# An attention and mixture-of-experts kernel: how the probabilities are split and transposed, and how the rotation changes halves

## The chip, the cores and the metric

The kernel runs on 1 core of one Trainium2 chip. The metric is device time in microseconds (us). Before the change three runs took 737.32, 738.01 and 740.93 us; their median is 738.01 us.

## The reference, cut to what matters

`x` is (4, 512, 256). After a layer norm it goes through an attention with 16 query heads and 4 key/value heads of width 128, and through a small mixture of experts; the result is `x + s * silu(ffn)`. The part that the change touches is the attention:

```python
q = q * cos + _rotate_half(q) * sin        # rotate_half: [-x2, x1], halves of 64 change places
k = k * cos + _rotate_half(k) * sin
q = q * xscale;  k = k * (1.0 / xscale)
scores = jnp.einsum('bhqd,bhkd->bhqk', q, k) / scale
scores = jnp.where(causal[None, None], scores, -jnp.inf)
attn = jax.nn.softmax(scores, axis=-1)
out = jnp.einsum('bhqk,bhkd->bhqd', attn, v)
out = out.transpose(0, 2, 1, 3).reshape(B, S, N_HEADS * HEAD_DIM)
return out @ Wo
```

All is float32 in the reference. The kernel keeps precision by splitting each float32 matrix into a float16 part ("hi") and a bfloat16 rest ("lo") and by adding three products: hi·hi, hi·lo, lo·hi.

## The kernel before, in words

The program has two stages. The attention comes first: 16 rounds (4 batches times 4 key/value heads), and in each round 4 heads that share keys and values, so 64 heads. The experts come second, and only their loads overlap the end of the attention.

One head needs scores of 512 queries against 512 keys, causal, so 10 of 16 blocks of 128x128: 1280 columns. They are handled in three units, `SCORE_UNITS`: unit 0 has 512 columns, unit 1 has 384 + 128, unit 2 has 256. For a head the steps are:

- TensorE (`score`, L1390) writes the scores of a unit to one of 3 PSUM banks. It waits until ScalarE has read that bank for the head before (`exped`).
- VectorE (`row_max`, L1096) adds the causal mask and takes the negated row maximum.
- ScalarE (`exponentials`, L777) takes the exponential into SBUF, float32 (`probs`), with the row sums. VectorE inverts the sums (L1102).
- GpSimd (`divide`, L539) multiplies the probabilities by the inverted sums, four instructions a head.
- TensorE (`transpose_probs`, L1403) transposes the ten float32 blocks into two PSUM banks, in three units; ScalarE (`probs_hi`, L785) casts a unit to float16 and VectorE (`probs_lo`, L1108) subtracts to get the low part.
- TensorE (`weigh_values`, L1419) multiplies values by the transposed probabilities, 12 matmuls; ScalarE and VectorE split the output (L799, L1114).

A round also projects the queries and keys of the next round: five items, q0, q1, k, q2 and q3 (`project`, L1359), one of 512 columns each. An item is rotated as follows. VectorE multiplies by cos (L1078) and by sin twice, on 64 partitions each, where the result is written to the other half (L1082, L1083). GpSimd adds (`rotate_sum`, L526), ScalarE casts to float16 (`rotate_hi`, L765), GpSimd subtracts (`rotate_lo`, L533). The first scores of the next round wait for the low part of q0 and of k (`rot_lo`). The item v is projected once (L1374), and the output projection of the round before is four items (L1435), which VectorE adds up (L1121).

The order is written out by hand, one instruction list for each engine, each executed in order; a wait on a semaphore stops all that stands behind it on that engine. In the loop of TensorE: scores of head j+1, then (for j = 1 and 2) the transposes of head j, a projection, an output projection, the last transposes of head j, and the values of head j-1. At the round's end come q2, an output projection, the transposes of head 3, the values of head 2, the scores of the next round's head 0, q3, and the rest. SyncE issues only loads in the attention, none of them inside the steady loop of the rounds.

## Time and profile before

| what | value |
|---|---|
| median of 3 runs | 738.01 us |
| span of the profiled execution | 735.7 us |
| TensorE busy (matmul) | 659.1 us, 90% |
| VectorE busy | 581.6 us, 79% |
| GpSimd busy | 537.8 us, 73% |
| ScalarE busy | 442.3 us, 60% |
| scores of 64 heads, TensorE L1390 | 116.4 us |
| transposes of the probabilities, L1403 | 93.5 us in 640 matmuls |
| values, L1419 | 118.0 us |
| division, GpSimd L539 | 176.4 us in 256 instructions |
| product with sin in two halves, L1082 and L1083 | 55.4 and 54.7 us |
| all DMA traffic | 50.44 MB |

The profiled execution's span of 735.7 us is 2.3 us below the median of the timed runs; only the span stands beside it. The page divides the span into 40 slices of 18.4 us. TensorE is busy for nine tenths or more of most slices from the ninth to the thirtieth, which is the attention; the slices behind are the experts. A row of `timeline` begins with its start and its duration in us from the start of the span. Instructions of an engine overlap by their tail, so the time that one takes from its engine is the distance from its start to the next start.

### The profile page before, as it was taken

The page shows a single profiled execution, that of the slowest core. Times are in us where ns is not written, and L with a number is a line of the kernel's source. Part 1 is how long each engine was busy: PE and PEld are TensorE (multiplying, and loading weights), DVE is VectorE, ACT ScalarE, POOL GpSimd, SP SyncE. Part 2 cuts the span into 40 slices and gives each one's busy share as a digit, 9 for nine tenths or more (in the row PEclk, how much of TensorE's full clock was granted, in tenths as well). Part 3 has the DMA queues.
Part 4 walks back from the last instruction along what each step waited for, and adds up shares of the span by engine and source line. Part 5 has one row for each costly group of instructions (what it writes and reads, how often), then busy time and mean ns, then how long its engine had stood idle before and what let it go on. Part 6 is the DMA issues. An engine that isn't in the chain of part 4 may idle for free.

```text
span 735.7 us, 17233 instructions
## 1 busy us (share of the span) xinstructions
PE 659.1 (90%) x4994; PEld 460.8 (63%) x4995; DVE 581.6 (79%) x1683; ACT 442.3 (60%) x1205; POOL 537.8 (73%) x588
## 2 busy tenths in 40 slices
PE   3678869789999999999999999999987899999992
PEld 1255546556766667676666766667665577767761
DVE  6988879789999999998999999999876344333378
ACT  3585636465657666575675657668584664555542
POOL 4677777978888887888877888888988993555510
PEclk9899989999999999999999999999998999999996
DMA  9491000500000000000000000000122564665772
GB/s 306 165 301 48 1 0 2 141 22 16 0 14 14 0 14 0 14 7 7 14 0 14 0 14 14 0 14 2 35 70 88 167 117 105 138 141 138 210 285 101
DMA packets 64952, 50.44 MB, mean 69 GB/s; under 512 B 35252, under 2 KB 58260, under 8 KB 64916
## 3 DMA queue, kind: packets, MB, share of 16 engines
q1 hardware_dynamic: 60804, 39.45, 19.3%
q0 software_dynamic: 3840, 10.52, 4.3%
q8 instruction: 20, 0.33, 0.2%
q14 instruction: 16, 0.13, 0.1%
q10 hardware_dynamic: 272, 0.02, 0.0%
HBM read 24.72 MB, written 18.96 MB: 59 GB/s over the span
## 4 chain that ended last, share of the span: by engine, by line
POOL 41%; issue 19%; PE 17%; DVE 13%; ACT 7%; DMA 2%; POOLq 0%; SPq 0%; DVEq 0%
POOL arena L539 16%; PE bank L1546 8%; POOL arena L533 8%; POOL arena L526 7%; PE bank L1576 6%; POOL xs_dram L586 4%; ACT arena L777 3%; POOL compare L582 2%; PE bank L1555 2%; DVE arena L1108 2%; POOL arena L563 1%; ACT arena L785 1%; DVE arena L1082 1%; DVE arena L1083 1%; DVE arena L1078 1%
## 5 line engine op out<-in xcount | busy, mean ns | idle before, releaser
L539 POOL TENSOR_TENSOR arena<-arena,rinv 128x128 f32<-128x128 f32 (+3 forms) x256 | 176.4, 720 | 83.5 <-DVE rinv L1102 83.4
L777 ACT ACTIVATE arena<-bank,nmax 128x512 f32<-128x512 f32 (+3 forms) x256 | 132.5, 535 | 64.6 <-DVE nmax L1096 64.6
L1096 DVE CUSTOM_DVE_ANT_0 bank<-bank,mask_b 128x512 f32<-128x512 f32 (+3 forms) x256 | 118.1, 516 | 14.2 <-issue 14.2
L1390 PE MATMUL bank<-arena 128*128 128x512 f16 (+7 forms) x768 | 116.4, 302 | 5.9 <-POOL arena L533 5.9
L785 ACT CAST arena<-bank 128x512 f16<-128x512 f32 (+1 forms) x192 | 93.3, 522 | 45.1 <-PE bank L1403 43.5
L1359 PE MATMUL bank<-xnT_hi,arena 128*128 (+1 forms) x320 | 111.0, 389 | 9.2 <-DVE arena L1083 4.7
L1419 PE MATMUL bank<-arena 128*128 128x512 f16 (+7 forms) x768 | 118.0, 305 | 0.0
L1403 PE MATMUL bank<-ident_f,arena 128*128 128x128 f32 x640 | 93.5, 277 | 25.5 <-DVE arena L1108 14.5
L1108 DVE TENSOR_TENSOR arena<-bank,arena 128x512 bf16<-128x512 f32 (+1 forms) x192 | 109.0, 595 | 3.9 <-ACT arena L785 1.8
L526 POOL TENSOR_TENSOR arena<-arena 128x512 f32<-128x512 f32 x77 | 98.6, 1281 | 2.5 <-DVE arena L1083 2.2
L1403 PEld LDWEIGHTS bank<-ident_f,arena 128*128 128x128 f32 x640 | 74.0, 142 | 38.9 <-DVE arena L1108 18.3
L1390 PEld LDWEIGHTS bank<-arena 128*128 128x128 f16 (+1 forms) x768 | 66.2, 98 | 48.1 <-issue 7.9
L533 POOL TENSOR_TENSOR arena<-arena 128x512 bf16<-128x512 f32 x80 | 92.5, 1161 | 4.8 <-ACT arena L765 4.8
L1435 PE MATMUL bank<-arena 128*128 (+2 forms) x768 | 94.6, 274 | 1.6 <-DVE logit L1048 1.2
L1419 PEld LDWEIGHTS bank<-arena 128*128 128x128 f16 (+1 forms) x768 | 68.3, 99 | 38.3 <-issue 2.4
L1435 PEld LDWEIGHTS bank<-arena 128*128 (+2 forms) x768 | 75.3, 98 | 19.9 <-issue 1.7
L1283 DVE TENSOR_TENSOR arena<-bank,arena 128x176 f32<-128x176 f32 x80 | 27.2, 340 | 73.3 <-ACT arena L912 71.8
L718 POOL DMA_INDIRECT ys_dram<-arena,row_u x48 | 46.0, 959 | 51.2 <-ACT arena L923 51.2
L765 ACT CAST arena<-arena 128x512 f16<-128x512 f32 x80 | 50.3, 629 | 53.9 <-POOL arena L526 49.3
L1359 PE MATMUL bank<-xnT_lo,arena 128*128 (+1 forms) x160 | 61.9, 387 | 0.0
L1359 PEld LDWEIGHTS bank<-xnT_hi,arena 128*128 (+1 forms) x320 | 31.9, 100 | 45.5 <-issue 8.3
L1082 DVE TENSOR_TENSOR arena<-bank,tab 64x512 f32<-64x512 f32 x80 | 55.4, 693 | 2.2
(147 smaller groups left out, 1158.9 us busy)
## 6 DMA issues: line engine op xcount, KB each, us to landing
xs_dram<-s_sb SPq DMA_DIRECT2D x4, 1548.0 KB, 14.4
stage<-w_gate_up SPq DMA_DIRECT2D x16, 352.0 KB
arena<-ys_dram SPq DMA_DIRECT2D x8, 512.0 KB, 6.5
stage<-w_down SPq DMA_DIRECT2D x16, 176.0 KB
stage<-wq SPq DMA_DIRECT2D x4, 512.0 KB, 8.0
stage<-wo SPq DMA_DIRECT2D x4, 512.0 KB, 6.5
stage<-x SPq DMA_DIRECT2D x1, 2048.0 KB, 10.6
out<-s_sb SPq DMA_DIRECT2D x8, 256.0 KB, 2.1
```

Of the source, the lines that this page charges most:

```text
L526: pool.tensor_tensor(rot_a[buf], rot_a[buf], rot_b[buf], ALU.add).then_inc(rot_add, 1)
L533: pool.tensor_tensor(dst, rot_a[buf], hi, ALU.subtract).then_inc(rot_lo, 1)
L539: ins = pool.tensor_tensor(pr, pr, rinv[:, par, qt:qt + 1].to_broadcast([P, (qt + 1) * P]), ALU.mult)
L777: ins = act.activation(probs[par][:, P_AT[qt]:P_AT[qt] + n], score_bank[u][:, col:col + n], ACT.Exp, scale=-1.0, bias=nmax[:, par, qt:qt + ...
L785: act.copy(pT[j % 2][0][:, at:at + cols], pt_bank[(3 * j + u) % 2][:, 0:cols]).then_inc(pt_hi, 1)
L1096: ins = dve.tensor_tensor_reduce(score_bank[u][:, col:col + n], score_bank[u][:, col:col + n], mask_b[:, S - n:S], -1.0, 3e38, ALU.add, AL ...
L1108: dve.tensor_tensor(pT[j % 2][1][:, at:at + cols], pt_bank[(3 * j + u) % 2][:, 0:cols], pT[j % 2][0][:, at:at + cols], ALU.subtract).then_ ...
L1359: ins = pe.matmul(ps[:], w[a][:, c * chunk:c * chunk + DH], tokens[m][:, c * TOK:c * TOK + S], start=(c == 0 and n == 0), stop=(c == KC - ...
L1390: ins = pe.matmul(score_bank[u][:, col:col + n_k], qT[a][:, j * S + qt * P:j * S + (qt + 1) * P], kT[m][:, 0:n_k], start=(n == 0), stop=(n ...
L1403: ins = pe.transpose(pt_bank[(3 * j + u) % 2][:, col + (qt - kt) * P:col + (qt - kt + 1) * P], probs[j % 2][:, P_AT[qt] + kt * P:P_AT[qt] ...
L1419: ins = pe.matmul(o_bank[:, kt * P:S], v_s[a][:, kt * DH:(kt + 1) * DH], pT[j % 2][m][:, PT_AT[kt]:PT_AT[kt] + n_q], start=(kt == 0 and n ...
L1435: ins = pe.matmul(ps[:, 0:D], heads[a][:, j * S + q * P:j * S + (q + 1) * P], w[m][:, j * D:(j + 1) * D], start=(j == 0 and n == 0), stop= ...
```

## The change: what it does

The row sums are inverted as before, but the division on GpSimd is gone. ScalarE takes the exponential in place in PSUM. Then it writes the high half of the probabilities to SBUF in float16, scaled by the inverted sum (`probs_hi`, four instructions a head), and VectorE computes the low half from PSUM in one `scalar_tensor_tensor` per block row (`probs_lo`, four a head). Both halves are then transposed: the high half by four transposing DMAs a head (10 blocks in all) from SyncE's queue (`transpose_hi`), the low half in 16 bits by TensorE, into a single PSUM bank in two units; ScalarE copies these to SBUF (`pT_lo_out`). The scores have 4 banks instead of 3, and a bank is free once the low half is computed, not once the exponential is taken. In the rotation VectorE multiplies by sin in one instruction of 128 partitions, into one buffer `rot_c`; two DMAs of 64 partitions (`swap_halves`) put the halves in their new places, and GpSimd's sum waits for them. The prologue's rotations stay as they were. SyncE's queue now runs through the rounds too, and the loads of the experts stand between them.

```diff
-PT_UNITS = [[(0, 0)], [(1, 0), (3, 384)], [(2, 0)]]
+PT_UNITS = [[(0, 0), (1, 512), (3, 896)], [(2, 0)]]
-PT_UNIT_COLS = [(0, 512), (512, 512), (1024, 256)]
+PT_UNIT_COLS = [(0, 1024), (1024, 256)]
+SCORE_BANKS = 4
...
+            def transpose_hi(rd, j):
+                h, par = rd.head(j), j % 2
+                if not (isinstance(h, int) and h < 2):
+                    sp.wait_ge(pv, h - 1)
+                for u, unit in enumerate(SCORE_UNITS):
+                    sp.wait_ge(p_hi_ready, h * 3 + u + 1)
+                    sp.sem_inc(hi_seen)
+                    for qt, _ in unit:
...
+                        sp.dma_start_transpose(dst, p_hi[par][:, P_AT[qt]:P_AT[qt] + n].bitcast(BF16)).then_inc(pT_hi_in[par], 16)
+            def swap_halves(rd, name):
+                sp.wait_ge(misc_free, rd.item(name))
+                sp.sem_inc(hi_seen)
+                sp.wait_ge(rot_add, rd.rot(name) - SWAP_BACK[name])
+                half, buf = DH // 2, SWAP_BUF[name]
+                sp.dma_start(rot_b[buf][0:half, :], rot_c[half:DH, :]).then_inc(swapped, 16)
+                sp.dma_start(rot_b[buf][half:DH, :], rot_c[0:half, :]).then_inc(swapped, 16)
...
+            def round_(rd):
+                for j in range(GH - 1):
+                    transpose_hi(rd, j + 1)
+                    if not rd.last:
+                        swap_halves(rd, ("q0", "q1", "k")[j])
...
+                if not rd.last:
+                    swap_halves(rd, "q2")
+                    transpose_hi(rd, GH)
+                    swap_halves(rd, "q3")
...
-            def divide(h, par):
-                pool.wait_ge(inverted, h + 1)
-                for qt in range(QT):
-                    pr = probs[par][:, P_AT[qt]:P_AT[qt] + (qt + 1) * P]
-                    ins = pool.tensor_tensor(pr, pr, rinv[:, par, qt:qt + 1].to_broadcast([P, (qt + 1) * P]), ALU.mult)
-                ins.then_inc(normed, 1)
...
+            def probs_hi(rd, j):
+                h, par = rd.head(j), j % 2
+                act.wait_ge(inverted, h + 1)
+                if not (isinstance(h, int) and h < 2):
+                    act.wait_ge(pT_hi_in[par], hi_landed(rd, j - 2))
+                for u, unit in enumerate(SCORE_UNITS):
                     for qt, col in unit:
                         n = (qt + 1) * P
+                        ins = act.activation(p_hi[par][:, P_AT[qt]:P_AT[qt] + n], score_at(j, u)[:, col:col + n], ACT.Copy,
+                                             scale=rinv[:, par, qt:qt + 1])
+                    ins.then_inc(p_hi_ready, 1)
+
+            def pT_lo_out(h, j, units):
                 for u in units:
                     at, cols = PT_UNIT_COLS[u]
-                    act.wait_ge(pt_ps, h * 3 + u + 1)
-                    act.copy(pT[j % 2][0][:, at:at + cols], pt_bank[(3 * j + u) % 2][:, 0:cols]).then_inc(pt_hi, 1)
+                    act.wait_ge(pt_ps, h * 2 + u + 1)
+                    act.copy(pT_lo[j % 2][:, at:at + cols], pt_bank[:, 0:cols]).then_inc(pt_lo, 1)
...
+                    exponentials(h, j + 1)
+                    pT_lo_out(rd.head(j), j, (0,))
+                    probs_hi(rd, j + 1)
...
+            def rotate_products(rd, name, freed, lows):
+                ps, buf = misc_bank[rd.bank(name)], ROT_BUF[name]
...
+                dve.tensor_tensor(rot_a[buf], ps[:], tab[:, cos, :], ALU.mult)
+                if lows is not None:
+                    probs_lo(*lows, (0,))
+                if not (rd.first and name == "q0"):
+                    dve.wait_ge(swapped, rd.swap(name) - SWAP_DMAS)
+                dve.tensor_tensor(rot_c, ps[:], tab[:, sin, :], ALU.mult).then_inc(misc_free, 1)
...
+                    for qt, col in SCORE_UNITS[u]:
+                        n, at = (qt + 1) * P, P_AT[qt]
+                        ins = dve.scalar_tensor_tensor(p_lo[par][:, at:at + n], score_at(j, u)[:, col:col + n], rinv[:, par, qt:qt + 1],
+                                                       p_hi[par][:, at:at + n], ALU.mult, ALU.subtract)
+                    ins.then_inc(p_lo_ready, 1)
...
-                    if reuse:
-                        pe.wait_ge(exped, h * 3 + u - 2)
+                    if not (isinstance(h, int) and h * 3 + u < SCORE_BANKS):
+                        pe.wait_ge(p_lo_ready, h * 3 + u - (SCORE_BANKS - 1))
...
-                    if not first or j > 0 or u == 2:
-                        pe.wait_ge(pt_lo, h * 3 + u - 1)
+                    if not first or j > 0 or u > 0:
+                        pe.wait_ge(pt_lo, h * 2 + u)
```

Before, SyncE's queue has no row inside the loop of the rounds. Now it has these; this piece is the loop's third head (the transposes of head 3's high half), the swap of k and the swap of q2:

```order
L477 ISA [waits pv]
L482 DMA_TRANSPOSE arena<-arena 128x4x128 [waits p_hi_ready]
L477 REGISTER_ALU
L482 DMA_TRANSPOSE arena<-arena 128x3x128 [waits p_hi_ready]
L482 DMA_TRANSPOSE arena<-arena 128x1x128
L477 REGISTER_ALU
L482 DMA_TRANSPOSE arena<-arena 128x2x128 [waits p_hi_ready]
L485 REGISTER_ALU
L487 REGISTER_ALU [waits misc_free]
L489 DMA arena<-arena 64x512 [waits rot_add]
L490 DMA arena<-arena 64x512
```

`pv` counts the heads whose values TensorE has weighed. The two DMAs of k's swap stand behind the four transposing ones and so behind their wait.

ScalarE in the loop, for j = 1, before (L785 are the casts of the transposed probabilities, L777 the exponentials of the next head):

```order
L785 CAST arena<-bank4 128x512 [waits pt_ps]
L785 CAST arena<-bank3 128x512 [waits pt_ps]
L774 ISA
L777 ACTIVATE arena,rsum<-bank0,nmax 128x512 [waits maxed]
L774 REGISTER_ALU
L777 ACTIVATE arena,rsum<-bank1,nmax 128x384 [waits maxed]
L777 ACTIVATE arena,rsum<-bank1,nmax 128x128
L774 REGISTER_ALU
L777 ACTIVATE arena,rsum<-bank2,nmax 128x256 [waits maxed]
```

and after (L843 the exponentials, L863 the copy of the low half transposed by TensorE, L855 the high half):

```order
L843 ACTIVATE bank2,rsum<-bank2,nmax 128x512 [waits maxed]
L840 REGISTER_ALU
L843 ACTIVATE bank3,rsum<-bank3,nmax 128x384 [waits maxed]
L843 ACTIVATE bank3,rsum<-bank3,nmax 128x128
L840 REGISTER_ALU
L843 ACTIVATE bank0,rsum<-bank0,nmax 128x256 [waits maxed]
L862 ISA
L863 COPY arena<-bank4 128x1024 [waits pt_ps]
L849 REGISTER_ALU
L851 ISA [waits inverted]
L855 ACTIVATE arena<-bank2,rinv 128x512 [waits pT_hi_in0]
L855 ACTIVATE arena<-bank3,rinv 128x384
```

What ScalarE does after its exponentials now stands in front of what VectorE waits for.

VectorE in the loop, for j = 2, behind the row maxima of head 3, before (L1108 the low parts, L1078 to L1083 the products of k):

```order
L1108 TENSOR_TENSOR arena<-bank3,arena 128x512 [waits pt_hi]
L1108 TENSOR_TENSOR arena<-bank4,arena 128x512 [waits pt_hi]
L1075 REGISTER_ALU
L1077 REGISTER_ALU [waits misc_ps]
L1078 TENSOR_TENSOR arena<-bank7,tab 128x512 [waits rot_lo]
L1102 RECIPROCAL rinv<-rsum 128x4 [waits exped]
L1082 TENSOR_TENSOR arena<-bank7,tab 64x512
L1083 TENSOR_TENSOR arena<-bank7,tab 64x512
```

and after (L1201 the low halves, L1154 and L1159 the products):

```order
L1190 RECIPROCAL rinv<-rsum 128x4 [waits exped]
L1152 REGISTER_ALU
L1153 REGISTER_ALU [waits misc_ps]
L1154 TENSOR_TENSOR arena<-bank7,tab 128x512 [waits rot_lo]
L1197 ISA
L1201 SCALAR_TENSOR_TENSOR arena<-bank1,rinv,arena 128x512 [waits p_hi_ready,pt_ps]
L1158 ISA
L1159 TENSOR_TENSOR arena<-bank7,tab 128x512 [waits swapped]
L1201 SCALAR_TENSOR_TENSOR arena<-bank2,rinv,arena 128x384 [waits p_hi_ready]
L1201 SCALAR_TENSOR_TENSOR arena<-bank2,rinv,arena 128x128
L1201 SCALAR_TENSOR_TENSOR arena<-bank3,rinv,arena 128x256 [waits p_hi_ready]
```

The low halves belong to the head whose maxima have just been taken; before, they belonged to the head ahead of it.

## Rows read from the trace of the kernel before

**Rows 1.** The page: span, and busy us of each engine with its instructions.

```profile
span 735.7 us, 17233 instructions
...
PE 659.1 (90%) x4994; PEld 460.8 (63%) x4995; DVE 581.6 (79%) x1683; ACT 442.3 (60%) x1205; POOL 537.8 (73%) x588
```

**Rows 2.** `windows`, one steady round: length, busy us of PE, PEld, DVE, ACT, POOL.

```profile
412.35:443.88 31.53, 31.03 (x242) 21.67 (x239) 29.03 (x85) 20.14 (x58) 25.82 (x30) 1.00 0.02 8
```

**Rows 3.** Timeline of PE: start us, duration us, engine, line, operation.

```profile
429.85 1.04 PE L1403 MATMUL bank<-ident_f,arena 128*128 128x128 f32 x8
430.72 1.79 PE L1419 MATMUL bank<-arena 128*128 128x512 f16 x12
432.68 1.80 PE L1390 MATMUL bank<-arena 128*128 128x512 f16 x12 [0.17 <-POOL arena L533]
...
437.14 1.79 PE L1390 MATMUL bank<-arena 128*128 128x512 f16 x12
...
442.69 0.22 PE L1374 MATMUL bank<-arena,xnT_lo 128*128 x1
442.74 0.28 PE L1374 MATMUL bank<-arena,xnT_hi 128*128 x2
...
444.64 1.79 PE L1390 MATMUL bank<-arena 128*128 128x512 f16 x12
...
451.60 1.79 PE L1390 MATMUL bank<-arena 128*128 128x512 f16 x12
```

**Rows 4.** Timeline of DVE, one head of the same round.

```profile
438.93 0.69 DVE L1096 CUSTOM_DVE_ANT_0 bank<-bank,mask_b 128x512 f32<-128x512 f32 x1
...
440.77 0.69 DVE L1078 TENSOR_TENSOR arena<-bank,tab 128x512 f32<-128x512 f32 x1
...
444.82 0.68 DVE L1114 TENSOR_TENSOR arena<-bank,arena 128x512 f32 x1
445.42 0.68 DVE L1087 TENSOR_TENSOR arena<-bank,arena 128x512 bf16<-128x512 f32 x1
446.02 0.41 DVE L1108 TENSOR_TENSOR arena<-bank,arena 128x256 bf16<-128x256 f32 x1
446.36 0.70 DVE L1096 CUSTOM_DVE_ANT_0 bank<-bank,mask_b 128x512 f32<-128x512 f32 x1
```

**Rows 5.** Timeline of ACT, the same head.

```profile
439.72 0.69 ACT L777 ACTIVATE arena<-bank,nmax 128x512 f32<-128x512 f32 x1 [2.35 <-DVE nmax L1096]
...
441.84 1.07 ACT L785 CAST arena<-bank 128x512 f16<-128x512 f32 x2
442.79 0.65 ACT L765 CAST arena<-arena 128x512 f16<-128x512 f32 x1
```

**Rows 6.** Timeline of POOL, the end of a round.

```profile
429.05 1.26 POOL L526 TENSOR_TENSOR arena<-arena 128x512 f32<-128x512 f32 x1
430.28 2.26 POOL L533 TENSOR_TENSOR arena<-arena 128x512 bf16<-128x512 f32 x2
```

**Rows 7.** `source` of L480, ns min/median/max on SyncE; timeline of SyncE: one plain DMA.

```profile
L480 SPq DMA_TRANSPOSE arena<-xs_dram x48: 1188/1193/4862, 593.6 to 689.1; - x48
...
561.51 0.42 SPq L470 DMA_DIRECT2D stage<-w_down  x1
```

**Rows 8.** `dma`: size and median us from issue to landing.

```profile
out<-s_sb SPq DMA_DIRECT2D x8, 256.0 KB, 2.1
...
stage<-shared_down SPq DMA_DIRECT2D x1, 96.0 KB, 3.7
```

**Rows 9.** `dma` of 630 to 660 us: queue q1, in which 16 transposing DMAs ran.

```profile
q1 hardware_dynamic: 8704, 2.10, 41.6%
```

**Rows 10.** Timeline of PE around its longest wait.

```profile
98.54 0.69 PE L1403 MATMUL bank<-ident_f,arena 128*128 128x128 f32 x2 [4.39 <-DVE arena L1108]
99.02 3.41 PE L1419 MATMUL bank<-arena 128*128 128x512 f16 x12
```

**Rows 11.** `windows` around it: PE busy, granted clock, DMA share.

```profile
96.00:100.00 4.00, 1.46 (x5) 0.55 0.00 0
```

266 lines of the change are left out of this document (150 added, 116 removed).

## The prediction

> **What bounds the kernel now.** I read the page first. The span is 735.7 us and TensorE is busy for 659.1 of it [rows 1]. Then I read one steady round in the windows: TensorE is busy for 31.03 of 31.53 us, VectorE for 29.03, GpSimd for 25.82, ScalarE for 20.14, and the DMA share is 0.02 [rows 2]. So the attention is bound by TensorE's work, with VectorE close behind. Each engine works through its list in order, and the timelines show how the lists interlock. The scores of heads 0, 1, 2 and 3 start at 432.68, 437.14, 444.64 and 451.60 [rows 3]; the steps are 4.46, 7.50 and 6.96 us, and 12.61 remain of the round to the next head 0. That last step is the path of k: k's rotation has to come back before the next head 0 can be scored. It is nearly late already, since the scores at 432.68 waited 0.17 us for GpSimd's low part (L533) [rows 3]. Two loops must therefore be watched besides busy time: head to head, and k's path once a round.
>
> **What the change takes from the busy engines.** Eight float32 transposes take 0.87 us of TensorE (429.85 to 430.72), 0.109 each [rows 3]; there are 40 in a round, 4.35 us. The trace has no 16-bit transpose. Its bounds are 0.055, the pitch of 16-bit matmuls of 128 columns (442.69, 442.74) [rows 3], and the same 0.109. I take 0.055, since shape and operand width agree: 2.2 us saved a round, TensorE at 28.9. VectorE loses one of the two products of 0.7 us with sin, five times a round, 3.5 us; the other becomes one instruction of 512 columns at 0.60 (444.82 to 445.42) [rows 4]. The low half is four instructions in place of three. From 0.60 for 512 columns and 0.34 for 256 (446.02 to 446.36) [rows 4], a column costs 1.0 ns and an instruction 0.08 us, so 384, 128 and 256 columns take 0.47, 0.21 and 0.34: 1.62 a head against 1.54. If the three-operand form lasts as long as the row maximum of 512 columns, 0.69 us [rows 4], it is 0.1 us more an instruction. VectorE comes to about 26 us. ScalarE gains four scaled copies a head and its transposed copies stay: about 27 us. GpSimd drops to 13. No engine is full after the change, so by busy time alone a round would take 28.9 us. What decides is the order.
>
> **The head-to-head loop.** Before, VectorE's low part belonged to the previous head, and a score bank was free after the exponential. Now VectorE takes the maxima of a head, then waits for ScalarE, which takes the exponentials, copies the previous head's transposed low half (1024 columns) and only then writes the high half; then VectorE computes the low half, and only behind that, in order, the next maxima. The two engines alternate and little of it overlaps. The link, from the start of one head's maxima to the next head's:
>
> - maxima to the end of the exponentials: 438.93 [rows 4] to 441.84 [rows 5], 2.91. ScalarE now writes to PSUM; I take the same.
> - the copy of 1024 columns: two casts of 512 take 441.84 to 442.79 [rows 5], 0.95.
> - first high half, 512 columns: 0.6 (the cast at 442.79 lasts 0.65 [rows 5]).
> - low half of unit 0, 0.60; product with sin, 0.60; low halves of units 1 and 2, 1.02 [rows 4].
> - one addition of a projection of 256 columns, 0.34 [rows 4].
>
> That is 7.02, and with three hand-offs of some 0.04 us 7.1. It holds from head 2 to head 3. From head 1 to head 2 VectorE has the output's and v's low parts, 1.20, in place of the addition: 8.0. From head 0 to head 1 ScalarE has a cast of 512 columns, half of 0.95, and a copy of 256, some 0.3, in place of 0.95: 6.9. Before, these steps took 6.96, 7.50 and 4.46. The division, 2.75 us a head on GpSimd, was beside other work and its going is worth nothing here.
>
> **The path of k, once a round.** TensorE's projection of k no longer decides. The swap's DMAs stand in SyncE's queue behind the transposing DMAs of head 3, and those wait for `pv` of head 1, because they overwrite the buffer that head 1's values are read from. Head 1's values stand behind the last two transposes of head 2, and these need the single PSUM bank, which ScalarE frees with the copy of 1024 columns behind head 3's exponentials. From the start of head 3's maxima:
>
> - to the end of the exponentials 2.91, the copy 0.95;
> - two transposes 0.11, head 1's values with their tail 1.79 [rows 3];
> - four transposing DMAs on SyncE's queue. Before shows one of four blocks: 1.193 us of the queue [rows 7]. A plain DMA takes 0.42 [rows 7], so I split this into 0.45 and 0.185 a block; 10 blocks in four DMAs are 3.65. The ends: 4 x 1.19 = 4.8 if the cost is the same for any size, and 1.9 if only data counts: q1 took 41.6% of 30 us for 16 transposes of 128 KB, 0.78 each [rows 9], for 320 KB 1.9;
> - the second swap DMA starts 0.45 later and lands after 2.1 us, as a store of 256 KB does; a small one took 3.7 [rows 8]. Take 2.1, bounds 2.1 and 3.7;
> - GpSimd: the sum 429.05 to 430.28, 1.23; then the low part of q1, which stands ahead, and that of k, two in 2.26 [rows 6];
> - the first scores until VectorE can start, 0.8, half of their 1.79 [rows 3].
>
> The sum is 2.91 + 0.95 + 1.90 + 3.65 + 0.45 + 2.1 + 1.23 + 2.26 + 0.8 = 16.25, with eight hand-offs 16.6, where before the step was 12.61. TensorE has some 4.7 us to do behind head 1's values (q2, an output projection, transposes, head 2's values) and then waits about 5 us for k. Such a wait has a second price: after its wait of 4.39 us at 98.54 the values took 3.41 instead of 1.79 us [rows 3, 10], and the granted clock from 96 to 100 us was 0.55 [rows 11], near the lower of the clock's two levels, 1.2 GHz. I put 0.7 us a round on it, the first scores at half speed beyond what VectorE's first maxima hide. VectorE is stopped too: its sin product of q2 reuses `rot_c` and waits for k's swap, but it has nothing on this path.
>
> **The sum.** 6.9 + 8.0 + 7.1 + 16.6 + 0.7 = 39.3 us a round against 31.53, 7.8 more. Fifteen rounds have a path of k: +117 us. The experts' stage begins later by as much and is otherwise the same, since its loads have more time than before. The profiled execution would go from 735.7 to about 853; the median of the runs shown is 2.3 higher, 855. I forecast 855 us. With 1.9 for the transposes, exponentials into PSUM 0.25 us a head shorter and no loss of clock, a round is 35.9, +66 us, 804. With 4.8 us, 3.7 to landing and 0.1 us more an instruction on VectorE it is 43.3, +177 us, 915. The likeliest case's own range is 810 to 905.
>
> **A rule of the skill.** The one row on a DMA transpose reads from HBM, 128 x 512 elements, four blocks in 1.193 us of queue and 0.78 us of data [rows 7, 9]. The Trainium skill (VectorE: DVE Perf Modes, "Rules for kernel authors") says to transpose 128x128 on TensorE if a PSUM destination is acceptable and by the crossbar DMA otherwise, and its section "The three transpose paths" gives 390 ns for TensorE and 1309 ns for the DMA. Before transposes at 109 ns a block, so the page's figure for TensorE is not met here; if its DMA figure held for each block in a row of them, a head's ten would take 13.1 us, more than a head takes now, by an estimate from that page about 1140 us for the whole. The Trainium skill also says (Advanced Engine Details and Errata, "X-Bar Transpose (TRN2)") that transposing DMAs are as fast as regular ones; by that the term of 3.65 would shrink toward its lower bound and the time toward 825. No row of before has a source in SBUF, so neither is settled by it.
>
> **Rivals.** First, the queue becomes the bound: each block read from SBUF costs what the whole four-block DMA cost, 1.19 us [rows 7]. A head needs 11.9 us of SyncE's queue and a round 47.6 + 5 x 0.9 = 52.1 us, 20.6 more; over 16 rounds 1065 us. For it: no row shows a source in SBUF. Against it: 1.193 covers four blocks. Chance with anything above 915: 0.09. Second, faster: the two loops are covered, because ScalarE and VectorE really overlap across units and the swap is back in time; TensorE's 28.9 us would bound, 2.6 less a round, 16 x 2.6 = 42, 696 us. It decides from the point at which a round's four links sum to less than 31.5, and they would have to lose 7.1 of 38.6. For it speaks only busy time [rows 2]. Chance 0.04. Third, no change: the losses of k's path (4.0) hold but the other links gain, 31.5 again, 738 us: 0.02. Fourth, a mild loss: k's path is 3 to 4 us shorter than summed (DMAs in parallel, low landing), a round of 33 to 35.5 us, 760 to 800 us: 0.06.
>
> **How the numbers follow.** The forecast of 855 has 0.79 within 804 to 915. The range for 8 in 10 is 808 to 920: below it lie the second to fourth rivals and above it the first. What a measurement can tell from no change is about 0.5%, 3.7 us. Faster 0.04, same 0.02, slower 0.94.
>
> **What would show it.** Right: in a steady round TensorE is busy for some 29 us of 38 to 40, with one wait of about 5 us before L1481 released by GpSimd's L610 (`rot_lo`), a fallen clock behind it; VectorE's L1201 waits for ScalarE's L855, and ScalarE's L843 for VectorE's maxima, each about once a head; SyncE waits for `pv`; GpSimd's L603 waits for a DMA. Wrong: if score starts are under 7 us apart and the wait for `rot_lo` is under 1 us; if SyncE's queue is busy all the time (the first rival); or if L482 issues take under 0.3 us each and the round is still long, in which case the step is elsewhere, in VectorE's and ScalarE's alternation.

## The result, and the profile after

The changed kernel takes 940.45 us (median of 4 runs, 938.77 to 941.97) against 737.86 us (737.32 to 740.93) of the kernel before: a ratio of 1.2735, 95% interval 1.2703 to 1.2766. The forecast was 855 us with a range of 808 to 920. The direction was right and the size was not: the kernel is 203 us slower, not 117.

The page of the kernel after, span and busy times, answers to [rows 1]; under it the windows of one steady round (length, busy us of PE, PEld, DVE, ACT, POOL, then granted clock, DMA share, GB/s), which answers to [rows 2].

```profile
span 938.3 us, 18321 instructions
...
PE 676.6 (72%) x4930; PEld 433.9 (46%) x4995; DVE 547.5 (58%) x1672; ACT 544.3 (58%) x1397; POOL 365.0 (39%) x332
```

```profile
464.08:508.46 44.38, 31.28 (x235) 19.52 (x238) 27.08 (x83) 26.45 (x69) 15.06 (x13) 0.96 0.28 65
```

The busy times came out near the forecast: VectorE 27.1 us a round (about 26 was worked out), ScalarE 26.5 (27), GpSimd 15.1 (13; by the prediction's own 2.75 us a head it would have been 14.8). TensorE shows 31.3 instead of 28.9. About 1.0 of that goes with the lower clock (0.96 on the mean): rope_engines below, with the same list on TensorE, shows 30.3 at a clock of 1.00. The transposes themselves are as quick as was taken: eight start at 488.94 and the next work at 489.39, 0.056 us each. The other 1.4 us is probably the way busy time is counted, which takes in the tail of the last matmul of every stretch; this was not followed up. No engine is busy for more than 31.3 of 44.38 us. The time went into waits, as the page of waits of the kernel after shows (engine, what, line, releaser: us in all, times, longest):

```profile
POOL arena L603 <- DMA arena<-arena: 359.7, 71, 16.8
ACT arena L832 <- POOL arena L603: 159.9, 40, 13.5
ACT bank L843 <- DVE nmax L1184: 125.4, 71, 5.6
...
DVE arena L1159 <- DMA arena<-arena: 85.2, 29, 10.2
...
PE bank L1481 <- POOL arena L610: 77.1, 16, 9.1
```

GpSimd's `rotate_sum` (L603) waits for the swap's DMAs, and it passes the wait on: to ScalarE, whose `rotate_hi` (L832) stands in one list with the exponentials and the output's high half, and to TensorE's scores (L1481). VectorE's sin product (L1159) waits for the swap before, because `rot_c` is one buffer.

Heads are best compared by the starts of their row maxima. Here are those of heads 0 to 3 and the next head 0 in the timeline of VectorE after (start us, duration us), to which 438.93 and 446.36 of [rows 4] answer:

```profile
464.08 0.69 DVE L1184 CUSTOM_DVE_ANT_0 bank<-bank,mask_b 128x512 f32<-128x512 f32 x1 [0.94 <-issue]
...
471.99 0.70 DVE L1184 CUSTOM_DVE_ANT_0 bank<-bank,mask_b 128x512 f32<-128x512 f32 x1
...
481.49 0.69 DVE L1184 CUSTOM_DVE_ANT_0 bank<-bank,mask_b 128x512 f32<-128x512 f32 x1
...
488.89 0.70 DVE L1184 CUSTOM_DVE_ANT_0 bank<-bank,mask_b 128x512 f32<-128x512 f32 x1
...
508.47 0.69 DVE L1184 CUSTOM_DVE_ANT_0 bank<-bank,mask_b 128x512 f32<-128x512 f32 x1 [0.94 <-issue]
```

The links are 7.91, 9.50, 7.40 and 19.58 us; the same starts before (433.55, 438.93, 446.36, 453.47, 465.06) give 5.38, 7.43, 7.11 and 11.59. The last link holds 8.0 of the 12.9 us a round. Its chain in the timeline after, rows of several engines put in order of time:

```profile
491.81 1.02 ACT L863 COPY arena<-bank 128x1024 bf16<-128x1024 bf16 x1
492.88 0.28 PE L1494 MATMUL bank<-ident_b,arena 128*128 128x128 bf16 x2 [0.72 <-ACT arena L863]
494.09 0.71 PE L1512 MATMUL bank<-arena 128*128 128x512 bf16 x4
495.01 5.21 SPq L482 DMA_TRANSPOSE arena<-arena  x4
500.47 0.46 SPq L489 DMA_DIRECT2D arena<-arena  x1
500.98 0.59 SPq L490 DMA_DIRECT2D arena<-arena  x1
503.34 1.26 POOL L603 TENSOR_TENSOR arena<-arena 128x512 f32<-128x512 f32 x1 [5.96 <-DMA arena<-arena]
504.56 2.26 POOL L610 TENSOR_TENSOR arena<-arena 128x512 bf16<-128x512 f32 x2
506.97 2.74 PE L1481 MATMUL bank<-arena 128*128 128x512 f16 x9 [5.00 <-POOL arena L610]
```

It is the chain that the prediction named: the copy of the transposed low half frees TensorE's transposes, head 1's values end, `pv` lets SyncE issue the four transposing DMAs of head 3, k's swap stands behind them, then landing, GpSimd's sum, two low parts, the scores. What it got wrong stands in the lines: the four DMAs hold the queue for 5.2 us, where 3.65 was taken. The slow scores behind the wait (nine matmuls in 2.74 us) had been forecast.

The second loss is in the link from head 1 to head 2 (timeline after, POOL, ACT, DVE):

```profile
477.55 1.26 POOL L603 TENSOR_TENSOR arena<-arena 128x512 f32<-128x512 f32 x1 [8.07 <-DMA arena<-arena]
...
478.85 0.62 ACT L832 CAST arena<-arena 128x512 f16<-128x512 f32 x1 [1.23 <-POOL arena L603]
479.37 0.58 ACT L877 CAST arena<-bank 128x512 f32 x1
...
480.27 0.69 DVE L1208 TENSOR_TENSOR arena<-bank,arena 128x512 f32 x1 [0.90 <-ACT arena L877]
```

The swap of q3 stands in SyncE's queue behind the four transposing DMAs of the new head 0 (5.19 us from 469.21 on) and is issued from 474.66 on. It comes back late, so ScalarE's cast of q3 is late, the cast of the output (L877) stands behind it in ScalarE's list, and VectorE's low half of the output (L1208) stands ahead of head 2's maxima. Such a chain was not in the prediction.

Over the whole run the last head's maxima start 208.4 us later (755.40 instead of 546.97), and what follows is 5.8 us shorter. Of the 208.4, 15 rounds account for 201.2, of which 15 x 12.87 = 193.0 by the steady round, and the last three heads add 6.9. The remaining 8.2 lie in the first four rounds, above all in the first (58.4 us against 38.7, with GpSimd's longest wait, 16.8) and the fourth (53.3 against 34.5); the second loses less than a steady one, 7.9. There other transfers stand ahead of a swap in SyncE's queue, as swap_only below shows.

### The profile page after: what moved, and what is told of

The parts are those of the page before. It is cut to its first block, busy times and chain, and to the rows that moved or that the text cites. A ratio compares the mean times of both kernels' runs of the same rounds, so it can differ in the third digit from the quotient of the medians.

```text
span 938.3 us, 18321 instructions
## 1 busy us (share of the span) xinstructions
PE 676.6 (72%) x4930; PEld 433.9 (46%) x4995; DVE 547.5 (58%) x1672; ACT 544.3 (58%) x1397; POOL 365.0 (39%) x332
## 4 chain that ended last, share of the span: by engine, by line
issue 39%; POOL 15%; ACT 13%; PE 13%; DVE 9%; SPq 6%; DMA 3%; ACTq 0%; POOLq 0%; DVEq 0%
PE bank L1639 6%; POOL arena L603 6%; ACT bank L843 4%; SPq L482 4%; PE bank L1669 4%; POOL arena L610 4%; ACT arena L855 3%; POOL xs_dram L655 3%; ACT arena L863 2%; POOL arena L632 2%; DVE arena L1201 2%; DMA arena<-arena 2%; ACT arena L832 1%; PE bank L1648 1%; SPq L507 1%
## 5 line engine op out<-in xcount | busy, mean ns | idle before, releaser
L603 POOL TENSOR_TENSOR arena<-arena 128x512 f32<-128x512 f32 x77 | 98.4, 1277 | 361.9 <-DMA arena<-arena 359.7
L1481 PE MATMUL bank<-arena 128*128 128x384 f16 (+2 forms) x763 | 147.1, 337 | 117.3 <-POOL arena L610 77.1
L843 ACT ACTIVATE bank<-bank,nmax 128x512 f32<-128x512 f32 (+3 forms) x256 | 127.7, 499 | 125.6 <-DVE nmax L1184 125.4
L1481 PEld LDWEIGHTS bank<-arena 128*128 128x128 f16 (+1 forms) x768 | 69.9, 108 | 183.3 <-issue 80.2
L1201 DVE SCALAR_TENSOR_TENSOR arena<-bank,rinv,arena 128x512 bf16<-128x512 f32 (+3 forms) x256 | 128.3, 545 | 41.8 <-ACT arena L855 41.7
L832 ACT CAST arena<-arena 128x512 f16<-128x512 f32 x80 | 50.3, 628 | 164.7 <-POOL arena L603 159.9
L855 ACT ACTIVATE arena<-bank,rinv 128x512 f16<-128x512 f32 (+3 forms) x256 | 115.8, 557 | 0.7 <-DVE rinv L1190 0.7
L1494 PE MATMUL bank<-ident_b,arena 128*128 128x128 bf16 x640 | 58.6, 224 | 60.7 <-ACT arena L863 60.7
L1159 DVE TENSOR_TENSOR arena<-bank,tab 128x512 f32<-128x512 f32 x75 | 51.5, 687 | 86.5 <-DMA arena<-arena 85.2
L863 ACT COPY arena<-bank 128x1024 bf16<-128x1024 bf16 (+1 forms) x128 | 90.1, 704 | 0.6 <-PE bank L1494 0.5
L1508 PE MATMUL bank<-arena 128*128 128x512 f16 (+3 forms) x512 | 84.1, 310 | 1.5 <-DVE arena L1208 1.5
L1494 PEld LDWEIGHTS bank<-ident_b,arena 128*128 128x128 bf16 x640 | 42.8, 100 | 83.1 <-ACT arena L863 69.5
L1208 DVE TENSOR_TENSOR arena<-bank,arena 128x512 f32 (+1 forms) x64 | 44.1, 690 | 60.7 <-ACT arena L877 60.7
L785 POOL DMA_INDIRECT ys_dram<-arena,row_u x48 | 46.0, 959 | 49.9 <-ACT arena L1000 49.9
## 6 DMA issues: line engine op xcount, KB each, us to landing
xs_dram<-s_sb SPq DMA_DIRECT2D x4, 1548.0 KB, 15.1
```

What stands on the lines that cost most here:

```text
L603: pool.tensor_tensor(rot_a[buf], rot_a[buf], rot_b[b], ALU.add).then_inc(rot_add, 1)
L843: ins = act.activation(p, p, ACT.Exp, scale=-1.0, bias=nmax[:, j % 2, qt:qt + 1], accum_out=rsum[:, j % 2, qt:qt + 1])
L855: ins = act.activation(p_hi[par][:, P_AT[qt]:P_AT[qt] + n], score_at(j, u)[:, col:col + n], ACT.Copy, scale=rinv[:, par, qt:qt + 1])
L863: act.copy(pT_lo[j % 2][:, at:at + cols], pt_bank[:, 0:cols]).then_inc(pt_lo, 1)
L1201: ins = dve.scalar_tensor_tensor(p_lo[par][:, at:at + n], score_at(j, u)[:, col:col + n], rinv[:, par, qt:qt + 1], p_hi[par][:, at:at + n] ...
L1481: ins = pe.matmul(score_at(j, u)[:, col:col + n_k], qT[a][:, j % GH * S + qt * P:j % GH * S + (qt + 1) * P], kT[m][:, 0:n_k], start=(n == ...
```

## Experiments

Two theories and two rivals were on record. Theory Q: what costs is the place of the swap in SyncE's queue, behind transposing DMAs. Theory A: VectorE and ScalarE take turns on one head. Rivals: D, the data that the transposing DMAs move slow things in general; L, the landing of a swap costs wherever it stands. Four more came with single runs: F and B (a transposing DMA's price on the queue is fixed, or goes by blocks), W (the queries' swaps hold the round as much as k's) and K (the clock behind TensorE's wait). All times are medians; before took 738 to 740 us beside them.

**rope_engines.** The rotation as in the kernel before, all else as after.

```diff
-                dve.tensor_tensor(rot_c, ps[:], tab[:, sin, :], ALU.mult).then_inc(misc_free, 1)
+                dve.tensor_tensor(rot_b[buf][0:half, :], ps[half:DH, :], tab[half:DH, sin, :], ALU.mult)
+                dve.tensor_tensor(rot_b[buf][half:DH, :], ps[0:half, :], tab[0:half, sin, :], ALU.mult).then_inc(misc_free, 1)
...
-                        swap_halves(rd, ("q0", "q1", "k")[j])
```

> The changed kernel, but the rotation's halves change places as before: VectorE multiplies by sin crosswise with two instructions into three rot_b buffers, and no swap DMA is left. In a steady round of the changed kernel (44.38 us) the starts of the row maxima are 7.91, 9.50, 7.40 and 19.57 us apart. Theory Q (the swap stands in SyncE's queue behind transposing DMAs): from head 3 to the next head 0 the wait for pv, 5.2 us of transposing DMAs, 0.9 of issue and 2.3 of landing leave the path of k, and ScalarE's and VectorE's waits for the swap (159.9 and 85.2 us in all) go; VectorE's longer sin product costs 0.8 us a head. A round of 36 to 39 us, 815 to 860 us in all, against 940. Theory A (VectorE and ScalarE alternate on a head, because the score bank comes free only after the low half, and that alone sets the round): the added 0.8 us a head on VectorE is on the path, 5 x 0.8 x 16 = 64 us more, 950 to 1005 us. Theory D (what costs is the data that the transposing DMAs move, beside everything else): no change within 2%, 920 to 955 us.

Measured: 858.2 us, ratio 1.160 (1.156 to 1.164). Links 8.23, 9.21, 8.35, 13.64, a round of 39.43, a little over the 36 to 39 expected; some rounds take 40.2. The last link lost 5.9 us although VectorE had more to do. A alone and D are out.

**swap_first.** The same instructions as after, but each swap ahead of the transposing DMAs in SyncE's list.

```diff
-                    transpose_hi(rd, j + 1)
                     if not rd.last:
                         swap_halves(rd, ("q0", "q1", "k")[j])
+                    transpose_hi(rd, j + 1)
...
                     swap_halves(rd, "q2")
+                    swap_halves(rd, "q3")
                     transpose_hi(rd, GH)
-                    swap_halves(rd, "q3")
```

> The changed kernel with the same instructions, but in SyncE's list each swap stands ahead of the head's transposing DMAs instead of behind them (q2's and q3's both ahead of the next head 0's). Theory Q: the swap's issue (0.9) and landing (2.3) stay, but the wait for pv and the 5.2 us of four transposing DMAs leave k's path; the transposes of a head start up to 1 us later. A round of 35 to 39 us, 800 to 860 us, some 10 to 20 us below or about the same as with the rotation on the engines, whose VectorE has 4 us more a round. Theory A: no change, 925 to 955 us. Theory D: no change, 925 to 955 us. A theory L (the swap's landing of 2.3 us and GpSimd's wait for it are the cost, wherever it stands): 0.9 + 2.3 us stay and only the queue's 5.2 us go where it counts, once a round: 15 x 5.2 = 78, about 862 us or more.

Measured: 844.2 us, ratio 1.141 (1.138 to 1.144). Links 7.91, 8.71, 7.40, 13.60; a round of 37.62. Nothing but the order in one queue was changed, and 96 of the 203 us went. It is below the 862 that theory L gave, so a landing is not the cost wherever it stands.

**one_transpose.** One transposing DMA of ten blocks a head. It waits for the high half of all three units, and TensorE weighs the values with it in matmuls of 128 columns.

```diff
-                    for qt, _ in unit:
...
-                        sp.dma_start_transpose(dst, p_hi[par][:, P_AT[qt]:P_AT[qt] + n].bitcast(BF16)).then_inc(pT_hi_in[par], 16)
+                sp.wait_ge(p_hi_ready, h * 3 + 3)
...
+                sp.dma_start_transpose(dst, p_hi[par][:].bitcast(BF16)).then_inc(pT_hi_in[par], 16)
```

> The changed kernel with one transposing DMA of ten blocks a head instead of four of one to four blocks; it waits for the high half of all three units, and the values' matmuls with the high half are ten of 128 columns a pass in place of four of 512 to 128 (the same columns). Theory Q with a fixed cost of 1.19 us of queue for each transposing DMA: four take 5.2 us and one takes 1.2 to 1.6, so k's path is 3.6 us shorter and the waits for q2's, q0's and q1's swaps shrink with it: a round of 36 to 40 us, 825 to 875 us. If the cost goes by blocks (0.45 and 0.185 a block, as the prediction split it), one takes 2.3 us against 3.65: 1.35 us a round, 915 to 925 us. If it goes by blocks alone (1.19 for four), 3.0 us for ten: 880 to 910. Theory A: the start is later by the wait for the last unit, not on VectorE's or ScalarE's path: no change, 925 to 950 us. Theory D: no change, the same bytes, 925 to 955 us.

Measured: 860.0 us, ratio 1.162 (1.158 to 1.166), links 7.91, 8.26, 7.40, 15.09. Of the expectations only that of a fixed price fits. The rows of the transposing DMAs in one_transpose and in the kernel after (ns min/median/max of one) show it:

```profile
L479 SPq DMA_TRANSPOSE arena<-arena x64: 1255/1324/8840, 35.5 to 679.8; - x64
```

```profile
L482 SPq DMA_TRANSPOSE arena<-arena x256: 1177/1190/6742, 33.3 to 765.4; - x128
```

**swap_only.** The kernel before with the swap by DMA and nothing else of the change.

```diff
-                dve.tensor_tensor(rot_b[buf][0:half, :], ps[half:DH, :], tab[half:DH, sin, :], ALU.mult)
-                dve.tensor_tensor(rot_b[buf][half:DH, :], ps[0:half, :], tab[0:half, sin, :], ALU.mult).then_inc(misc_free, 1)
+                    dve.wait_ge(swapped, rd.swap(name) - SWAP_DMAS)
+                    dve.tensor_tensor(rot_c, ps[:], tab[:, sin, :], ALU.mult).then_inc(misc_free, 1)
```

> The kernel before with one part of the change alone: the sin product is one instruction into rot_c and two DMAs on SyncE's queue swap the halves; probabilities are divided, transposed in float32 on TensorE and split as before. Nothing stands ahead of a swap in SyncE's queue. Each round has 3.5 us less on VectorE and k's path has 0.9 of issue and 2.3 of landing more, less 0.8 of the product. Before, k's low part was 0.17 us late in a round of 31.53. Theory Q: a landing alone costs little: k's projection came some 3 us ahead of GpSimd's sum of k, which hides most of it: 738 to 765 us. Theory L (the landing is the cost wherever it stands): 15 x 2.4 = 36 us and a lost clock in each round behind the wait, 775 to 800 us. Theory A: 730 to 740 us, VectorE is relieved and nothing alternates.

Measured: 751.7 us, ratio 1.015 (1.012 to 1.019). The windows of a steady round of swap_only:

```profile
449.20:480.54 31.34, 30.64 (x240) 21.70 (x239) 25.17 (x79) 20.15 (x57) 25.83 (x30) 1.00 0.20 50
```

The round is as long as before (31.5) with VectorE at 25.2 instead of 29.0 us: relieving VectorE was worth nothing, TensorE held the round. The 12 us lie in the first round (49.4 us against 38.7) and the fourth (39.7 against 34.5). That nothing stands ahead of a swap, as the expectation says, is not so there. In the first round it is four stores of 1548 KB each from another part of the program (SyncE and GpSimd in swap_only):

```profile
45.04 11.47 SPq L474 DMA_DIRECT2D xs_dram<-s_sb  x4
56.62 5.00 SPq L457 DMA_DIRECT2D arena<-arena  x1
61.67 1.33 SPq L458 DMA_DIRECT2D arena<-arena  x1
68.06 1.26 POOL L568 TENSOR_TENSOR arena<-arena 128x512 f32<-128x512 f32 x1 [10.04 <-DMA arena<-arena]
```

GpSimd's wait of 10.0 us is about the 10.8 that the round lost. In the fourth round loads of the experts' weights fill the queue from 164.34 to 172.03 us, and GpSimd waits 4.8 us for the swap behind them. No run moved these transfers, so this is read from the trace and not tried; it is the same mechanism, a swap behind other DMAs in one queue, without a transposing one.

**k_engines.** After, with k alone rotated on the engines.

```diff
+                if name == "k":
...
+                    dve.tensor_tensor(rot_b[b][0:half, :], ps[half:DH, :], tab[half:DH, sin, :], ALU.mult)
+                    dve.tensor_tensor(rot_b[b][half:DH, :], ps[0:half, :], tab[0:half, sin, :], ALU.mult).then_inc(misc_free, 1)
+                    return
```

> The changed kernel with k alone rotated as before (two crosswise products on VectorE into rot_b, no swap DMA for k); the four queries keep their swaps, each still behind a head's transposing DMAs in SyncE's queue. Theory Q, k's path alone: the wait for pv, 5.2 us of transposing DMAs, 0.9 of issue and 2.3 of landing leave the path from head 3 to the next head 0, VectorE has 0.8 us more: that link falls from 19.57 to 13.6 us as where all five rotations went back to the engines or the swaps stood first, a round to 37 to 39 us, and with 7 us less in each of 15 rounds the kernel takes 835 to 860 us. Theory W (k's path is only a part, and ScalarE's and VectorE's waits for the queries' swaps, 159.9 and 85.2 us in all, hold the round as much): more than half of the gain stays away, 885 to 925 us. Theory A (alternation of VectorE and ScalarE on a head alone): 940 to 955 us.

Measured: 852.4 us, ratio 1.155 (1.152 to 1.158); links 7.29, 9.50, 7.40, 14.17. k's path carries nearly all of it. The link of 9.50 stays, as it must where it is the queries' swaps that are late; with the swap first or with one transposing DMA it fell to 8.7 and 8.3. (In rope_engines, without swaps, it is 9.2, because the sin products take longer there: its link without any late swap, from head 2 to head 3, is 0.95 longer too.)

**engines_and_one.** rope_engines and one_transpose together.

> The rotation on the engines as in the kernel before, and one transposing DMA of ten blocks a head. Alone the first gave 858.2 us and the second 860.0. Theory Q says that both take the same thing off k's path, the queue ahead of the swap; with no swap left the transposing DMAs only have to be back before the values, two heads later. So the two do not add: 845 to 865 us. If the gains were of different causes they would add, 80 + 82: about 780 us. Theory D (the transposing DMAs' load on anything beside the swap costs): clearly under 845.

Measured: 857.3 us, ratio 1.161 (1.158 to 1.163), a round of 39.72. The gains don't add: both took the same queue off k's path.

**order_as_before.** engines_and_one with the exponentials in SBUF and VectorE's maxima ahead of the low half. What comes with that changes too: three banks for scores and two for the low half's transposes, those transposes one head later, and one buffer instead of two for the high half and for the transposed low half.

```diff
-                        p = score_at(j, u)[:, col:col + (qt + 1) * P]
-                        ins = act.activation(p, p, ACT.Exp, scale=-1.0, bias=nmax[:, j % 2, qt:qt + 1], accum_out=rsum[:, j % 2, qt:qt + 1])
+                        n = (qt + 1) * P
+                        ins = act.activation(probs[j % 2][:, P_AT[qt]:P_AT[qt] + n], score_at(j, u)[:, col:col + n], ACT.Exp, scale=-1.0, bias=nmax[:, j % 2, qt:qt + 1], accum_out=rsum[:, j % 2, qt:qt + 1])
...
                     row_max(h, j + 1)
+                    probs_lo(rd.head(j), j, (0, 1, 2))
...
-                        pe.wait_ge(p_lo_ready, h * 3 + u - (SCORE_BANKS - 1))
+                        pe.wait_ge(exped, h * 3 + u - (SCORE_BANKS - 1))
```

> The rotation on the engines, one transposing DMA a head, and the order of the kernel before on VectorE: exponentials go to SBUF in float32 and so free the score bank (three banks for scores, two for the low half's transposes), the low half is computed behind the NEXT head's maxima, its transposes stand on TensorE one head later. The same arithmetic, split and DMAs. The low half overwrites the exponentials in place, the high half and the transposed low half have one buffer each. Theory A+Q (what is left above the kernel before once the swap's queue is gone, 39.4 us against 31.53 a round, is VectorE and ScalarE taking turns on one head): the steps from head to head fall to what VectorE and TensorE have to do, some 29 busy us a round, and a round takes 31 to 34 us: 735 to 775 us. If Theory A is wrong, the order changes nothing: 845 to 870 us. If the exponentials' place mattered more than the order (ScalarE writing float32 to SBUF), the exponentials of 512 columns, now 0.66 us, would be clearly longer and the time above 775.

Measured: 797.3 us, ratio 1.081 (1.075 to 1.087), 60 us less. Links 6.15, 8.95, 6.15, 13.02; windows of a round of order_as_before:

```profile
445.95:480.22 34.27, 29.87 (x289) 21.12 (x287) 30.22 (x90) 26.91 (x69) 15.15 (x13) 1.00 0.19 46
```

So the order of the kernel before, with all that comes with it, was worth 5.45 us a round (39.72 to 34.27); that it is the taking of turns alone was not separated. The total missed the upper end of 775. Of the 58 us above the kernel before, 24 lie in the first four rounds (177.5 us against 153.5), which the expectation took for steady ones. The exponentials' place is not the reason: those of 512 columns take 0.69 us in SBUF against 0.66 in PSUM. The steady round is 2.75 us above before. In it VectorE waits 3.8 us for ScalarE's cast of the output (at 459.84, 474.79 and 479.60), against 0.6 before; why the cast is late was not tried. A contention told in the last section adds 0.6.

**fill_wait.** After, with 20 thrown-away matmuls in TensorE's wait of 5 us, from the fourth round on.

```diff
+                        for _ in range(20):
+                            pe.matmul(score_at(GH, 0)[:], wkv_s[0][:, 0:DH], wkv_s[0][:, 0:S], start=True, stop=True)
                     score(rd.head(GH), GH, rd.rot("q0"), rd.rot("k"))
```

> The changed kernel with 20 matmuls of 512 columns, whose result is thrown away, on TensorE in the wait of 5 us ahead of the next head 0's scores, from the fourth round on (12 rounds). Nothing else is touched; they fill 4.3 us of a wait of 5. Theory K (the clock): the scores behind the wait ran at half clock, 3.11 us instead of 1.79, and VectorE's first maxima came 1.5 us after their start instead of 0.8; with TensorE kept busy the scores take 1.79 us again and each of 12 rounds gains 0.7 to 1.3 us: 924 to 932 us. If the clock has no part, or the filling itself delays the scores: 938 to 945 us.

Measured: 929.6 us, ratio 1.258 (1.255 to 1.260), below the 1.270 that is the lower end after. The timeline of TensorE in fill_wait and, for the same scores, in the kernel after:

```profile
454.25 4.48 PE L1583 MATMUL bank<-arena 128*128 128x512 f16 x20
459.34 1.80 PE L1481 MATMUL bank<-arena 128*128 128x512 f16 x12 [0.61 <-POOL arena L610]
```

```profile
462.58 3.11 PE L1481 MATMUL bank<-arena 128*128 128x512 f16 x12 [4.99 <-POOL arena L610]
```

Twelve matmuls take 1.80 instead of 3.11 us; the kernel before had shown the like once, behind 4.39 us of waiting [rows 10, 11]. The granted clock was 0.73 in the kernel after from 462.58 to 467.50, between its levels of 1.2 and 2.4 GHz on the mean, behind 5 us of idle TensorE, and 1.00 here. The round falls from 44.38 to 43.04: 0.71 in the last link and 0.63 in the first. Other rounds gain less (43.7); on the mean it is 0.9. Work that does nothing made the kernel 11 us faster.

**ten_transposes.** Ten transposing DMAs of one block a head; the same data.

```diff
+                        for kt in range(qt + 1):
...
+                            sp.dma_start_transpose(dst, p_hi[par][:, at:at + P].bitcast(BF16)).then_inc(pT_hi_in[par], 16)
```

> The changed kernel with each head's high half transposed by ten DMAs of one block instead of four of one to four blocks: the same blocks from the same source, into the same places. Theory F (a transposing DMA holds SyncE's queue for a fixed 1.19 us, whatever its size): ten take 11.9 us a head where four took 5.2 (4.8 by 1.19), k's path is 7 us longer and the queue has 47.6 + 4.5 us a round to issue, beside its waits: a round of at least 52 us and up to 60, 1060 to 1220 us. Theory B (the cost goes by blocks): 12.8 us would have been 3 to 5.2 us before too, so no change, 930 to 960 us.

Measured: 1334.6 us, one run, above what either theory expected: a round of 69.6 us. The timeline of SyncE in ten_transposes:

```profile
498.71 12.58 SPq L483 DMA_TRANSPOSE arena<-arena  x10
511.59 0.48 SPq L490 DMA_DIRECT2D arena<-arena  x1
```

That is 1.26 us a DMA with one block each, gaps included; the median is 1.23. Theory F holds; the expected time was too low, because it took the queue for a bound of its own, while the longer queue is also inside k's chain, and the clock falls to 0.75 over a round.

**first_and_one.** swap_first and one_transpose together.

> Swaps ahead of the transposing DMAs and one transposing DMA a head. Alone they gave 844 and 860 us. By theory Q both take away the queue ahead of the swap, so together they give little more than the better one. Still open in swap_first are the waits for a swap that stands behind the previous head's four transposing DMAs (GpSimd waits 229.5 us for swaps there): one transposing DMA leaves 1.3 us in place of 5.2. 825 to 845 us. If the rest is VectorE and ScalarE taking turns alone, 840 to 850; if the queue was still the bound, 790 to 820.

Measured: 822.3 us, ratio 1.113 (1.110 to 1.116), lower than expected for a queue that no longer counts. Links 7.29, 8.27, 7.41, 13.62, clock 1.00. The first two are 0.6 and 0.4 below swap_first's. There, q3's swap still stood behind four transposing DMAs: GpSimd waited 3.24 us for it until 484.75, and ScalarE's cast of q3, ahead of the copy and the high half, waited in its turn. In the link behind, the granted clock was 0.50 from 490.5 to 492.5 and the projection's matmuls, at 0.43 us from start to start instead of 0.22, were late. A round of 36.59 is the change without the waits in its queue.

**order_and_swap.** order_as_before with the queries swapped by DMA.

```diff
                 if not rd.last:
                     row_max(rd.head(GH), GH)
+                probs_lo(rd.head(3), 3, (0, 1, 2))
+                output_lo(rd, 2)
...
+                    if not rd.last and j < 2:
+                        swap_halves(rd, ("q0", "q1")[j])
```

> The order of the kernel before (797.3 us with all five rotations on the engines), with the four queries swapped by DMA again and k rotated by VectorE; the output's low half of head 2 stands behind the next head 0's maxima. VectorE has 0.8 us less for each query, 3.2 of 30.2 busy us a round, and waits no longer 1.66 us for head 2's output ahead of the maxima. If VectorE is what holds that order's round of 34.27 us, it falls to 31.5 to 33.5 us: 755 to 785 us. If ScalarE (26.9 busy us and in the chain with the high half, the copy of the transposed low half and the exponentials) holds it, 785 to 800 us. A swap that comes back late for a query shows as GpSimd's wait for a DMA and gives over 800.

Measured: 807.2 us, ratio 1.093 (1.090 to 1.097), worse than order_as_before. A round of 34.47 us with VectorE at 29.0: neither less work on VectorE nor the moved wait shortened it. The page shows 140.0 us of GpSimd's waits for swaps and 153.0 for ScalarE's casts; which of the two holds the round was not separated. No version here beats the kernel before.

## Why the prediction was right in direction and wrong in size

Each step, as the prediction put it, and what the traces show:

- **The busy times and "what decides is the order"**: right, within 2.4 us a round on each engine.
- **"maxima to the end of the exponentials 2.91, the copy 0.95, two transposes and head 1's values 1.90"**: right; from 488.89 the copy starts at 491.81, the transposes at 492.88, SyncE at 495.01, 6.1 in all against 5.8 and hand-offs.
- **"10 blocks in four DMAs are 3.65"**: the step that failed first. It took 5.2. I had split 1.193 us [rows 7] into 0.45 and 0.185 a block by the price of a plain DMA, without a row of another size. One block, one to four blocks and ten take 1.23, 1.19 and 1.32 us (medians of three runs): the queue's price is by the DMA. The bound of 4.8 was the truth, with some 0.15 us between each two. On this chain it is 1.55 us a round.
- **"lands after 2.1 us"**: 2.36 (500.98 to 503.34); small.
- **GpSimd 1.23 and 2.26**: right. So is 2.91 to the end of the exponentials; the 0.25 us a head that the lower end of the range took off for PSUM did not come (488.89 to 491.81 is 2.92).
- **"0.8 until VectorE can start" and "0.7 for the clock"**: 1.5 together (506.97 to 508.47), right in sum; fill_wait shows 0.71 of it to be the clock. What the step left out is the same slow clock one link later, 0.63.
- **"from head 1 to head 2 VectorE has ... 8.0"**: failed; 9.50. The link holds a swap, which the prediction looked for only on k's path. Its sentence that VectorE's wait for k's swap "has nothing on this path" is true of the last link and hid that the queries' swaps stop ScalarE ahead of the output's cast. This is the second step that failed, a wait that was left out. first_and_one, where no late swap stops ScalarE, gives 8.27.
- **"7.1" and "6.9"**: 7.40, and 7.29 without the clock: 0.3 and 0.4 short each.

A round was worked out as 39.3 and is 44.38 us. The 5.1 us are 2.3 in the last link (1.55 transposes, 0.26 landing, the rest hand-offs), 1.5 from head 1 to 2, 1.0 from head 0 to 1 and 0.3 from head 2 to 3. Times 15 this is 76 of the 86 us that were missed (203 against 117); the first rounds, taken for steady ones, are most of the rest. The transposes' term alone would not have saved the forecast: with 4.8 for it and the landing as measured the same sum gives 876. The experiments divide the 12.87 us that a round lost in another way: 7.8 are the waits in the swap's queue with the clock that they cost (44.38 to 36.59). What is left is 5.1. The order of the kernel before gives back 5.45 on the engines' version, but that version starts from 39.72 and ends at 34.27, so it doesn't show that all of the 5.1 is the taking of turns. The prediction had 4.7 for k's path and 3.1 for the other links.

The first rival, the queue as the bound with 1.19 us a block, did not come: a DMA of four blocks costs what one of one does. ten_transposes is that rival made real, and its time, 1335, is far above the 1065 that the rival was given: a queue inside a chain costs more than its sum. The second, third and fourth rivals (696, 738, 760 to 800 us) fell: each needed a shorter k's path or links than summed, and every link came out longer.

The Trainium skill (VectorE: DVE Perf Modes, "The three transpose paths") gives 1309 ns for a 128x128 transpose by DMA. The trace of ten_transposes has 1.26 us of the queue for such a DMA, near the page's figure, but 1.32 us for ten blocks in one: read as a price by block, the page's number is ten times too high here. Its advice in "Rules for kernel authors", to transpose on TensorE where PSUM will do, is what the kernel before follows, and no version with transposing DMAs beat it; no run put only these transposes back on TensorE, so the advice itself was not tried. The other page that was weighed, Advanced Engine Details and Errata, "X-Bar Transpose (TRN2)", calls transposing DMAs as fast as regular ones. For landing this agrees with up to four blocks, as the kernel after shows (size where known, median us from issue to landing); ten blocks in one DMA took 3.0 in one_transpose. For the queue it does not: 1.19 us against 0.46 and 0.59.

```profile
arena<-arena SPq DMA_DIRECT2D x150, 128.0 KB, 2.3
arena<-arena SPq DMA_TRANSPOSE x256, 2.3
```

## What to carry to other kernels

A DMA put into a queue is an instruction in a list: before asking how long it takes to land, ask what stands ahead of it, what that waits for, and how many DMAs hold the queue; here a change of order alone was worth 96 us and fewer, larger DMAs 80. When one resource turns up in several loops (a swap for k and for four queries), follow it in each of them, also through the engines that have only a cast behind it. Loads and stores of another stage in the same list count as well. Taking work off an engine that isn't the bound (VectorE before: 29.0 to 25.2 us, the round the same) buys nothing, and the order that the change needed for it, with two engines alternating on one head, cost some 5 us a round.

## What the runs showed of the hardware

- A transposing DMA from SBUF to SBUF held SyncE's queue for 1.19 us with one to four blocks of 128x128 in 16 bits, 1.23 as one of ten with one block each, and 1.32 with ten blocks (medians). A plain DMA of 128 KB within SBUF held it for 0.46 to 0.60 us.
- TensorE ran 12 matmuls in 3.11 us behind 5 us of idleness and in 1.80 us behind matmuls without use.
- VectorE's scalar_tensor_tensor took longer beside GpSimd when both its tensors lay in SBUF. By shape in order_as_before (both in SBUF) and in the kernel after (one in PSUM): count, busy us, mean ns over the whole run.

```profile
L1188 DVE SCALAR_TENSOR_TENSOR arena<-arena,rinv 128x512 bf16<-128x512 f32 x64 | 62.8, 981 | 0.0
```

```profile
L1201 DVE SCALAR_TENSOR_TENSOR arena<-bank,rinv,arena 128x512 bf16<-128x512 f32 x64 | 48.0, 751 | 41.8 <-ACT arena L855 41.7
```

In order_as_before four of them took 2.53 us from 488.13 on, beside a GpSimd sum at 487.65, and 1.94 us at 462.81, behind GpSimd's work:

```profile
462.81 1.94 DVE L1188 SCALAR_TENSOR_TENSOR arena<-arena,rinv 128x512 bf16<-128x512 f32 x4
...
487.65 1.27 POOL L592 TENSOR_TENSOR arena<-arena 128x512 f32<-128x512 f32 x1
488.13 2.53 DVE L1188 SCALAR_TENSOR_TENSOR arena<-arena,rinv 128x512 bf16<-128x512 f32 x4
```

ScalarE took exponentials beside both. In the kernel after three such instructions with a PSUM source took 1.26 us beside a GpSimd sum (at 478.11 and at 496.68) and 1.26 at 470.48 with GpSimd idle. The Trainium skill (GPSIMD Engine Reference, "Specifications") says that GpSimd shares its SBUF interfaces with VectorE and contends with instructions that have two SBUF inputs; the traces agree, with 0.6 us for these four. In a steady round of order_as_before one head of four is hit, so it explains 0.6 of the 2.75 us that this round is above before.
